# Twenty-six products that nobody reads, placed in waits of TensorE in a four-layer decoder

## The chip, the core and the metric

The kernel is one launch on one core of a Trainium2 chip. The metric is the device time of the launch in microseconds, the median of several runs. Five engines work beside each other: TensorE (PE in the rows; PEld is its load of a stationary operand), VectorE (DVE), ScalarE (ACT), GpSimd (POOL) and SyncE (SP), which issues the transfers. They meet by semaphores that the kernel's text names itself: every wait is written out by hand.

## The reference

Eight sequences of 128 tokens with 128 features pass through four layers. Each layer is an attention-like stage, a second stage that may look at a context, and a mixture of experts; each is added to `x` and gets the layer norm of `x`. All is float32.

```python
for layer in range(4):                      # 12 stages in a row
    x = x + attn[layer](layernorm(x))       # L1: a gated linear recurrence; L3: 10 chosen queries per head
    x = x + xattn[layer](layernorm(x), ctx) # L0, L1: softmax attention; L2: linear attention (elu + 1); L3: two products
    x = x + ffn[layer](layernorm(x))        # experts with 2 (L3: 1) of 8 chosen per token

# L0_xattn, the pattern of the softmax attentions: 16 heads of 8 features
q, k, v = split(x @ Wq.T), split(ctx @ Wk.T), split(ctx @ Wv.T)
scores = where(causal, q @ k.T / sqrt(8), -inf)
out = merge(softmax(scores) @ v) @ Wo.T
```

## The kernel before

**Layout.** `x` lies in SBUF as 128 tokens by 8 sequences times 128 features, and `ctxT` holds the context turned, 128 features by 1024 tokens. PSUM is used as eight tiles of 128x512 float32, `banks[0]` to `banks[7]`. A float32 product of 128x128 by 128x512 stands in the profile as two MATMUL rows of 128x512, so "x2" there is one such product.

**Order.** There is no scheduler. Each engine runs its functions in the order in which they are written, stage after stage, and an instruction whose wait is not met stops all that stands behind it on its engine. Some work of the next stage is written into the loops of the stage before (functions with `ahead` in the name).

**The attentions of layers 0 and 3** (`batches_pe`, line 915, and its partners on the other engines) loop over u = 0 to 9, one step per sequence and two to drain. At step u TensorE makes the scores of sequence u (four products with 32 rows each, L922, into banks 0 to 3), turns the exponentials of sequence u-1 (L939, banks 4 and 5), multiplies them by the values (L534, bank 6) and turns the sums back (L929). The scores of u wait for the masks of u-1 (`masked`, made by VectorE in L1037) in layer 0, and for `lowered` (VectorE, L1048) in layer 3. At u = 0 there is no u-1, so TensorE has nothing between the scores of the first sequence and those of the second. The hook `ahead(pe, u, "end")` is called at the end of each step.

**The recurrence of layer 1** (`layer1_recurrence_pe`, line 1829) mixes the recurrence's products with the key and value products of the next stage (`layer1_keys_values_pe(pe, i)`, L2023, i = 0 to 15) and its queries (L2030). Number 15 waits until ScalarE has emptied the bank that number 12 wrote (L2169). VectorE empties number 15 (L2171), then runs the scan of the recurrence (L1949 to L1955), and the recurrence's last product L1821 waits for that.

**The attention of layer 1** (`layer1_cross_pe`, line 2048) loops over v = 0 to 10, four heads of four sequences at a time. `EDGE_USES[v]` lists what else TensorE turns in step v (L2091): the values `("vh", n)` in steps 0, 2 and 3, and the results `("weighed", n)` in steps 6, 7 and 10. Each such group of four transposes into bank 7 waits until VectorE has emptied bank 7 of the last one (`freed`). In the list, n = 0 to 2 occur twice, as `vh` in step 0 and as `weighed` in steps 6 and 7.

**The second stage of layer 2** (`layer2_cross_pe`, line 2660) has a like loop: scores L2674, then sums of queries (L2683) and values (L2691). Its first scores wait for the queries, keys and values to be made positive and masked by VectorE, ScalarE and VectorE again.

**Layer 3's attention** gets its scores into `batches_pe` after a long stretch on VectorE that picks queries.

Of the kernel before, what the change touches and what calls it, by code (L numbers as in the profile page):

```python
# [21 lines left out]
BANK = 512  # L22
# [98 lines left out]
def build_program(nc, d, out):  # L121
    with ExitStack() as ctx:
# [179 lines left out]
        def turn_x_pe(pe, st, h, bank):  # L302
            n = norm[st]
            for j in range(4):
                b = 4 * h + j
                pe.wait_ge(*n["xc"](b + 1))
                o = pe.transpose(banks[bank][:, j * P:(j + 1) * P], xc[:, b, :], ident[:, :])
            o.then_inc(n["turned"].sem, 1)

        def keep_xnT(eng, who, st, h, bank):  # L310

# [1319 lines left out]


        def layer0_experts_ahead_pe(pe, u, point):
            if (u, point) == (7, "end"):
                pe.wait_ge(*a1s["masked"](4 * NB))
                turn_x_pe(pe, "L0_ffn", 0, 3)
            if (u, point) == (8, "heads back"):
                pe.wait_ge(*weights("L0_ffn"))
                pe.wait_ge(*norm["L0_ffn"]["xn0"](1))
                route_logits_pe(pe, e0, 0, W["L0_ffn_gate_w"][:, :], 2)  # L1640
            if (u, point) == (9, "heads back"):
                route_counts_pe(pe, e0, 0, 2)
# [182 lines left out]
        def layer1_recurrence_pe(pe):  # L1825
            pe.wait_ge(*weights("L1_attn"))
            recurrence_in_pe(pe, 0)
            pe.wait_ge(*weights("L1_xattn"))
            pe.wait_ge(*r1m[0].out(3))
            for i in range(4):  # L1830
                layer1_keys_values_pe(pe, i)
            recurrence_gates_pe(pe, 0)
            for i in range(4, 8):
                layer1_keys_values_pe(pe, i)
            turn_x_pe(pe, "L1_attn", 1, 2)
            pe.wait_ge(*r1m[0].out(7))
            recurrence_in_pe(pe, 1)
            recurrence_out_pe(pe, 0)
            for i in range(8, 12):
                layer1_keys_values_pe(pe, i)  # L1840
            recurrence_gates_pe(pe, 1)
            turn_x_pe(pe, "L1_xattn", 0, 4)
            for i in range(12, 16):
                layer1_keys_values_pe(pe, i)

            pe.wait_ge(*norm["L1_xattn"]["xn0"](1))
            pe.wait_ge(*r1m[1].out(7))
            layer1_queries_pe(pe, 0, 0)
            layer1_queries_pe(pe, 0, 1)
            pe.wait_ge(*kv1m.out(14))  # L1850
            layer1_queries_pe(pe, 0, 2)
            pe.wait_ge(*kv1m.out(15))
            layer1_queries_pe(pe, 0, 3)
            recurrence_out_pe(pe, 1)
# [180 lines left out]
        def layer1_cross_pe(pe):  # L2035
# [4 lines left out]
            for v in range(8 + 3):  # L2040
# [41 lines left out]
                for use, n in EDGE_USES[v]:  # L2082
# [8 lines left out]
                        o = pe.transpose(banks[7][:, j * P:(j + 1) * P], src, ident[:, :])  # L2091
                    o.then_inc(g["vh_turned" if use == "vh" else "heads_back"].sem, 1)
                    freed = g[use](n + 1)
                if v == 1:
                    pe.wait_ge(*kv1m.out(13))
                    turn_x_pe(pe, "L1_xattn", 1, 6)
# [562 lines left out]

        def layer2_cross_pe(pe):  # L2660
            g, m = c2g, c2m
            pe.wait_ge(*m.out(1))
            pe.wait_ge(*m.out(2))
            pe.wait_ge(*m.out(3))
# [362 lines left out]
        def layer3_attention_pe(pe):  # L3027
# [15 lines left out]
            pe.wait_ge(*g["wg_unit"](1))  # L3043
            pe.transpose(banks[7][0:GD, 3 * P:3 * P + NE], wg_unit[:, :], ident[0:NE, 0:NE]).then_inc(g["wg_turned"].sem, 1)
            pe.wait_ge(*g["wg_ready"](1))
            batches_pe(pe, a3s, a3h, a3["qT"], W["L3_attn_woT"][:, :], a3["vp"], "L3_attn", False, layer3_cross_ahead_pe)

        def layer3_attention_act(act):
# [172 lines left out]


        def layer3_cross_ahead_pe(pe, u, point):
            if (u, point) == (7, "end"):
                pe.wait_ge(*a3s["lowered"](3 * NB))
                pe.wait_ge(*a3s["exped"](4 * NB - 3))
# [314 lines left out]
```

## Time and profile before

| What | Value |
|---|---|
| Median of 3 runs | 1294.52 us (1293.5 to 1294.74) |
| The profiled execution, its own time | 1286.18 us |
| Span of its trace, first to last instruction | 1284.2 us |
| Mean granted TensorE clock | 0.896 of full speed |
| Busy: PE, PEld, DVE, ACT, POOL | 79%, 59%, 60%, 51%, 26% |
| DMA | 33 GB/s mean, 42.46 MB |

The granted clock is a share of 2.4 GHz: 1.00 is 2.4 GHz and 0.50 is 1.2 GHz, the only two levels; a value between them is a mix over the stretch. Times in rows are microseconds from the start of the span. The end of a row is its start plus its duration. The brackets at a row's end say how long the engine sat idle before it and who released it.

### The profile page before, as it was taken

What the parts mean: (1) busy time and instruction counts of PE and PEld (TensorE: products, weight loads), DVE (VectorE), ACT (ScalarE), POOL (GpSimd) and SP (SyncE); (2) the same over time, 40 slices, a digit from 0 to 9 for tenths busy, and PEclk for the clock granted to TensorE, in tenths of its full rate; (3) what the DMA queues carried; (4) which work ended last, traced back from release to release, by engine and by line L of the source; (5) the groups of instructions that cost most, each with busy time, mean ns of one, the idle gap of its engine ahead of it and who ended that gap; (6) DMA issues with size and microseconds to landing.
All of it is one profiled execution on the core that took longest, in us unless ns stands there. A gap on an engine that the chain in (4) does not pass through costs nothing. (4 is left out here: it accounts for less than half of the span.)

```text
span 1284.2 us, 22278 instructions
## 1 busy us (share of the span) xinstructions
PE 1010.8 (79%) x8221; PEld 758.4 (59%) x8221; DVE 771.8 (60%) x1870; ACT 656.8 (51%) x1688; POOL 337.2 (26%) x440
## 2 busy tenths in 40 slices
PE   6257877783779767779999989997789961878998
PEld 4224444352776355579976765775358850546898
DVE  4889995783323766752246665665777667764422
ACT  1168885561445646736538774775113223763433
POOL 2254542662222134410003331333410031111000
PEclk9689897896889778999999999999689995998999
DMA  7200000002555000020000000000120000000000
GB/s 246 85 1 1 2 1 18 1 1 66 150 166 198 1 1 2 2 99 1 1 2 1 2 2 1 2 2 33 79 107 26 1 1 0 2 1 1 1 1 17
DMA packets 31978, 42.46 MB, mean 33 GB/s; under 512 B 7592, under 2 KB 25632, under 8 KB 30592
## 3 DMA queue, kind: packets, MB, share of 16 engines
q1 hardware_dynamic: 30848, 38.95, 9.1%
q0 software_dynamic: 1024, 2.10, 0.5%
q8 instruction: 66, 1.08, 0.4%
q14 instruction: 40, 0.33, 0.1%
HBM read 35.54 MB, written 5.51 MB: 32 GB/s over the span
## 5 line engine op out<-in xcount | busy, mean ns | idle before, releaser
L1287 ACT ACTIVATE arena<-bank,w_L_ffn_b1T 128x512 f32<-128x512 f32 x128 | 86.9, 688 | 98.5 <-PE bank L1229 98.0
L1264 PEld LDWEIGHTS bank<-bufB,arena 128*128 128x128 f32 x1024 | 118.9, 192 | 2.4
L1264 PE MATMUL bank<-bufB,arena 128*128 128x128 f32 x1024 | 119.6, 275 | 0.0
L2525 ACT ACTIVATE arena<-arena 128x128 f32<-128x128 f32 x256 | 99.2, 390 | 20.0 <-DVE arena L2552 20.0
L293 POOL TENSOR_TENSOR norm_rstd<-norm_std,minus_half 128x4 f32<-128x4 f32 x24 | 25.4, 1060 | 316.0 <-DVE norm_std L288 316.0
L2536 POOL TENSOR_TENSOR arena<-arena 128x512 f32<-128x512 f32 x64 | 66.5, 1040 | 151.8 <-DVE arena L2585 151.8
L1324 DVE SCALAR_TENSOR_TENSOR x<-bank,gate_c,x 128x128 f32<-128x128 f32 x128 | 36.0, 344 | 114.9 <-PE bank L1264 114.7
L545 ACT ACTIVATE arena<-arena 128x128 f32<-128x128 f32 x256 | 80.3, 395 | 42.3 <-DVE arena L553 42.3
L1229 PE MATMUL bank<-x_high,w_low 128*128 128x512 f32 x200 | 85.7, 429 | 8.1 <-DVE w_low L1238 5.5
L1229 PE MATMUL bank<-x_high,w_high 128*128 128x512 f32 x200 | 81.1, 405 | 0.0
L1229 PE MATMUL bank<-x_low,w_high 128*128 128x512 f32 x200 | 81.0, 405 | 0.0
L2548 DVE SCALAR_TENSOR_TENSOR arena<-bank,bufA 128x512 f32<-128x512 f32 x64 | 43.8, 685 | 35.2 <-PE bank L2474 35.2
L2848 ACT ACTIVATE arena<-bank 128x512 f32<-128x512 f32 x36 | 21.6, 599 | 61.2 <-PE bank L1229 61.2
L514 PE MATMUL bank<-arena 128*128 128x512 f32 x64 | 37.3, 674 | 18.9 <-DVE arena L474 18.9
L2396 PE MATMUL bank<-xnT,bufA 128*128 128x512 f32 x96 | 50.7, 627 | 1.6 <-ACT arena L341 1.6
L341 ACT ACTIVATE arena<-bank 128x512 f32<-128x512 f32 x36 | 21.5, 596 | 58.7 <-PE bank L2396 39.3
L757 POOL TENSOR_TENSOR arena<-arena 128x512 f32<-128x512 f32 x32 | 33.8, 1057 | 64.4 <-DVE arena L876 64.4
L2445 PE MATMUL bank<-arena 128*64 128x128 f32 x512 | 42.1, 285 | 10.7 <-ACT arena L2516 10.5
L1229 PEld LDWEIGHTS bank<-x_high,w_low 128*128 128x128 f32 x200 | 39.4, 197 | 17.1 <-DVE w_low L1238 6.0
L2431 PEld LDWEIGHTS bank<-arena 128*128 128x128 f32 x256 | 36.7, 191 | 21.2 <-issue 14.1
L963 ACT ACTIVATE arena<-bank 128x512 f32<-128x512 f32 x64 | 36.7, 598 | 23.5 <-PE bank L939 23.1
L2525 ACT ACTIVATION_READ_ACCUMULATOR arena<-arena 128x1 f32 x256 | 48.3, 189 | 0.0
(489 smaller groups left out, 2555.6 us busy)
## 6 DMA issues: line engine op xcount, KB each, us to landing
bufB<-in_L_ffn_w SPq DMA_DIRECT2D x28, 256.0 KB
bufA<-in_L_ffn_w SPq DMA_DIRECT2D x2, 2048.0 KB, 9.8
bufB<-in_L_ffn_W SPq DMA_DIRECT2D x2, 2048.0 KB
bufB<-in_L_ffn_w SPq DMA_DIRECT2D x2, 2048.0 KB
bufA<-in_L_ffn_Wgu SPq DMA_DIRECT2D x1, 2304.0 KB, 9.0
bufA<-in_L_attn_Wqkv SPq DMA_DIRECT2D x1, 2048.0 KB, 8.8
rows<-blank SPq DMA_DIRECT2D x2, 960.0 KB, 6.9
results<-arena SPq DMA_DIRECT2D x6, 256.0 KB
```

The lines of the kernel that those rows point to most:

```text
L514: pe.matmul(banks[k % 2][:, :], qT[:, b * P:(b + 1) * P], m["kM"][k % 4].rearrange("p j t -> p (j t)"), start=True, stop=True).then_inc(s[ ...
L545: m = act.activation(tile[:, j * P:(j + 1) * P], tile[:, j * P:(j + 1) * P], ACT.Exp, bias=low[:, j:j + 1], scale=SCALE)
L963: act.activation(m["p"][n % 4], banks[4 + n % 2][:, :], ACT.Copy).then_inc(s["probs"].sem, 1)
L1229: m = pe.matmul(bank[:, :], a[:, ws], b[:, c], start=n == 0, stop=n == 2)
L1264: i = pe.matmul(bank[:, j * P:(j + 1) * P], h[:, f, j * P:(j + 1) * P], w2[:, u * FF + f * P:u * FF + (f + 1) * P], start=f == 0, stop=f = ...
L1287: act.activation(m["h"][k % 2][:, f, :], banks[f][:, :], ACT.Gelu, bias=b1[:, c:c + 1]).then_inc(g["hidden"].sem, 1)
L2396: o = pe.matmul(bank[:, :], w[:, c * P:(c + 1) * P], xnT[:, i * BANK:(i + 1) * BANK], start=True, stop=True)
L2431: o = pe.matmul(banks[7][:, u * P:(u + 1) * P], b2["oT"][k % 2][:, j * P:(j + 1) * P], b2_wo[:, c:c + P], start=False, stop=k == UNITS - 1 ...
L2445: o = pe.matmul(banks[5 + k % 2][64 * t:64 * t + 64, j * P:(j + 1) * P], b2["v"][gg % 2][:, 4 * u + 2 * j + r, :], b2["p"][(U0 + k) % 3][: ...
L2525: o = act.activation(tile, tile, ACT.Exp, bias=b2["mn"][n % 8][:, j:j + 1], scale=-1.0, accum_out=b2["sm"][n % 8][:, j:j + 1])
L2536: pool.tensor_tensor(tile, tile, bc(b2["rs"][n % 4], 2, P), ALU.mult).then_inc(g["over_sum"].sem, 1)
L2548: dve.scalar_tensor_tensor(tile, banks[r][:, :], -1.0 / np.sqrt(DH).item(), bias[:, h0:h0 + 4, :].rearrange("p h t -> p (h t)"), ALU.mult, ...
```

## The change

A helper makes `n` products of the identity by the first half of the context, 128x128 by 128x512 in float32, into a bank. It signals nothing and nobody reads the result. It is called at six places in the text: behind the scores of u = 0 in layers 0 and 3 (three products each), before key and value product 15 of layer 1 (five), behind each group of `EDGE_USES` with n below 3 (one each), and before the first scores of layer 2's second stage (nine). The last group runs six times, since n below 3 comes as `vh` and again as `weighed`, so 26 products are made in all. Two waits are written in for bank 6: `r1m[1].out(7)` before the five, and `a3m.out(4)` before layer 3's batches.

```diff
+        def keep_clock_pe(pe, bank, n):
+
+            for _ in range(n):
+                pe.matmul(banks[bank][:, :], ident[:, :], ctxT[:, 0:BANK], start=True, stop=True)
...
         def layer0_experts_ahead_pe(pe, u, point):
+            if (u, point) == (0, "end"):
+                keep_clock_pe(pe, 6, 3)
...
             turn_x_pe(pe, "L1_xattn", 0, 4)
-            for i in range(12, 16):
+            for i in range(12, 15):
                 layer1_keys_values_pe(pe, i)
+            pe.wait_ge(*r1m[1].out(7))
+            keep_clock_pe(pe, 6, 5)
+            layer1_keys_values_pe(pe, 15)
...
                     o.then_inc(g["vh_turned" if use == "vh" else "heads_back"].sem, 1)
                     freed = g[use](n + 1)
+                    if n < 3:
+                        keep_clock_pe(pe, 6, 1)
...
         def layer2_cross_pe(pe):
             g, m = c2g, c2m
+            keep_clock_pe(pe, 6, 9)
...
             pe.wait_ge(*g["wg_ready"](1))
+            pe.wait_ge(*a3m.out(4))
             batches_pe(pe, a3s, a3h, a3["qT"], W["L3_attn_woT"][:, :], a3["vp"], "L3_attn", False, layer3_cross_ahead_pe)
...
         def layer3_cross_ahead_pe(pe, u, point):
+            if (u, point) == (0, "end"):
+                keep_clock_pe(pe, 6, 3)
```

No other engine's order changes. On TensorE, at layer 1's attention in step v = 0, between the last scores and the scores of v = 1, this stood before (L2052 is a score, L2091 a transpose of values):

```order
L2052 MATMUL bank3<-bufA,arena 128x128
L2091 MATMUL bank7<-ident,bufA 128x128 x4
L2091 MATMUL bank7<-ident,bufA 128x128 [waits vh]
L2091 MATMUL bank7<-ident,bufA 128x128 x3
L2052 MATMUL bank0<-bufA,arena 128x128 [waits masked]
```

The second and third of these rows' pattern came three times there. Now (L2062 and L2101 are the same two lines, moved by the added text, and L313 is the helper's product):

```order
L2062 MATMUL bank3<-bufA,arena 128x128
L2101 MATMUL bank7<-ident,bufA 128x128 x4
L313 MATMUL bank6<-ctxT,ident 128x512
L2101 MATMUL bank7<-ident,bufA 128x128 [waits vh]
L2101 MATMUL bank7<-ident,bufA 128x128 x3
L2062 MATMUL bank0<-bufA,arena 128x128 [waits masked]
```

One product stands between a group of transposes and the next one's wait, three times. On TensorE in step v = 6 of the same loop the rows are now these (L2089 turns exponentials):

```order
L2089 MATMUL bank5<-ident,arena 128x128 x3
L2101 MATMUL bank7<-ident,bufA 128x128 [waits res,vh]
L2101 MATMUL bank7<-ident,bufA 128x128 x3
L313 MATMUL bank6<-ctxT,ident 128x512
L2101 MATMUL bank7<-ident,bufA 128x128 [waits weighed]
L2101 MATMUL bank7<-ident,bufA 128x128 x3
L313 MATMUL bank6<-ctxT,ident 128x512
L2062 MATMUL bank0<-bufA,arena 128x128 [waits masked]
```

The second L313 stands directly before the scores of v = 7; before the change the last transposes did.

## Rows read from the trace of the kernel before

**Rows 1.** The page, 40 equal slices of the span: TensorE's granted clock in tenths

```profile
PEclk9689897896889778999999999999689995998999
```

**Rows 2.** Windows: stretch, us, busy of PE, PEld, DVE, ACT, POOL, clock, DMA

```profile
230.50:240.70 10.20, 6.00 (x36) 3.20 (x36) 8.12 (x13) 4.69 (x8) 7.66 (x10) 0.50 0.01 2
240.80:288.40 47.60, 40.09 (x423) 24.10 (x420) 40.18 (x84) 34.67 (x67) 35.00 (x39) 1.00 0.00 1
466.10:493.20 27.10, 19.10 (x209) 15.45 (x212) 15.30 (x35) 9.04 (x18) 12.36 (x13) 0.50 0.01 1
899.60:913.00 13.40, 9.85 (x58) 4.52 (x58) 9.95 (x17) 1.15 (x3) 8.54 (x21) 0.50 0.40 170
1056.60:1097.40 40.80, 8.69 (x40) 4.33 (x41) 27.43 (x70) 14.80 (x22) 7.70 (x9) 0.50 0.00 0
```

**Rows 3.** Timeline, start of layer 0's second attention: start, us, engine, instruction, count

```profile
228.44 1.14 PE L922 MATMUL bank<-bufB 32*128 32x512 f32 x8 [1.48 <-DVE bufB L903]
234.70 2.09 PE L922 MATMUL bank<-bufB 32*128 32x512 f32 x8 [5.12 <-POOL bufB L903]
...
240.77 0.68 DVE L1037 TENSOR_TENSOR arena<-bank,causal 128x512 f32<-128x512 f32 x1
...
242.51 1.14 PE L922 MATMUL bank<-bufB 32*128 32x512 f32 x8
...
249.10 1.14 PE L922 MATMUL bank<-bufB 32*128 32x512 f32 x8
```

**Rows 4.** Timeline, end of layer 1's recurrence

```profile
441.62 7.11 PE L1811 MATMUL bank<-arena,w_L_attn_WgT 96*96 96x512 f32 x16
449.10 2.80 PE L2023 MATMUL bank<-ctxT,w_L_xattn_WvT 128*32 128x256 f32 x48
456.34 1.93 PE L2023 MATMUL bank<-ctxT,w_L_xattn_WvT 128*32 128x256 f32 x16 [4.44 <-ACT bufA L2169]
458.34 1.02 DVE L2171 TENSOR_TENSOR bufA<-bank,w_L_xattn_bv 128x512 f32<-128x512 f32 x1 [4.25 <-PE bank L2023]
464.15 2.13 PE L1821 MATMUL bank<-w_L_attn_WoT,arena 96*128 96x128 f32 x16 [1.88 <-DVE arena L1955]
```

**Rows 5.** Timeline, layer 1's attention, steps 0, 1, 6 and 7

```profile
473.35 1.11 PE L2091 MATMUL bank<-ident,bufA 128*128 128x128 f32 x4 [0.40 <-DVE arena L2198]
...
487.56 6.47 PE L2030 MATMUL bank<-xnT,w_L_xattn_WqT 128*32 128x128 f32 x128 [1.92 <-ACT xnT L341]
...
527.64 0.71 PE L2091 MATMUL bank<-ident,bufA 128*128 128x128 f32 x4 [0.90 <-DVE arena L2228]
528.29 1.17 PE L2052 MATMUL bank<-bufA,arena 8*128 8x128 f32 x32
529.48 0.69 DVE L2211 TENSOR_TENSOR arena<-bank,arena 128x512 f32<-128x512 f32 x1 [0.50 <-PE bank L2052]
```

**Rows 6.** Timeline, start of layer 2's second stage, and a later step

```profile
893.65 0.61 PE L2431 MATMUL bank<-arena 128*128 128x128 f32 x4
901.72 2.09 PE L2674 MATMUL bank<-bufB 32*128 32x512 f32 x8 [7.46 <-DVE bufB L903]
906.49 2.09 PE L2674 MATMUL bank<-bufB 32*128 32x512 f32 x8 [1.43 <-DVE arena L2772]
918.24 0.33 PE L2697 MATMUL bank<-ident,bufB 128*128 128x128 f32 x1 [2.24 <-DVE x L2786]
```

**Rows 7.** Timeline, layer 3's attention, and two full-width products at the lower clock

```profile
13.60 3.75 PE L349 MATMUL bank<-xnT,w_L_attn_Wq 128*128 128x512 f32 x4 [0.83 <-issue]
...
1085.00 2.09 PE L922 MATMUL bank<-arena 32*128 32x512 f32 x8 [1.20 <-DVE arena L903]
1092.38 2.09 PE L922 MATMUL bank<-arena 32*128 32x512 f32 x8 [5.29 <-DVE arena L1048]
```

**Rows 8.** Windows: a stretch with L2091 transposes alone, and the fall after 916.5

```profile
546.50:550.90 4.40, 2.37 (x16) 1.80 (x15) 1.65 (x6) 0.79 (x2) 0.00 (x0) 1.00 0.00 0
...
920.00:930.10 10.10, 7.91 (x80) 4.58 (x78) 7.21 (x13) 0.28 (x1) 4.86 (x15) 0.50 0.01 2
```

## The prediction

> **What bounds the kernel now.** I read first the page's slices, for TensorE's granted clock [rows 1]. A digit below 9 marks a slice in which part of the work ran at 1.2 GHz instead of 2.4. In the first half nearly every slice has some, in the middle none. The windows then say where the low stretches lie [rows 2]: 230.5 to 240.7 at the start of layer 0's second attention, 466.1 to 493.2 in layer 1's, 899.6 to 913.0 at the start of layer 2's second stage, 1056.6 to 1097.4 before and in layer 3's attention. In each the reader is to see a clock of 0.50, and beside it 1.00 in the steady part of the same attention, 240.8 to 288.4. Last I read the timeline for what TensorE did before each fall and for the duration of one instruction group at either level.
>
> The pattern is the same each time. TensorE waits for another engine: 5.12 us before 234.70 [rows 3], 4.44 us before 456.34 [rows 4], 7.46 us before 901.72 [rows 6], 5.29 us before 1092.38 [rows 7]. The work behind the wait is slow: eight score rows take 2.09 us at 234.70 and 1.14 us at 228.44 and 242.51 [rows 3]. Nothing else differs between them. So the change has to be priced by the work that follows each wait, at either clock, and only where another engine then waits for it.
>
> **What one product costs.** No row before has this very product. The nearest at 2.4 GHz is the eight products of L1811, 7.11 us for 16 rows, so 0.89 us each (96 rows of the array, the same 512 columns) [rows 4]. At 1.2 GHz it is L349: four rows, two products, 3.75 us, so 1.88 us each [rows 7]. All 26 together take about 23 us of TensorE at the high clock and 49 at the low one. What matters is whether they end before the wait they stand in.
>
> **Layer 0, three products.** The scores of u = 0 end at 229.58, the next start at 234.70 [rows 3]. At 2.4 GHz the products end at 229.58 + 3 x 0.89 = 232.25, hidden by 2.4 us. At 1.2 GHz they would end at 235.22, 0.5 us late. If the clock stays up, the scores of u = 1 take 1.14 instead of 2.09: 0.95 us, and VectorE masks those scores and paces what follows. More is possible: from 234.70 to 242.51 a step took 7.81 us, the next took 6.59 [rows 3], a difference of 1.22. And VectorE's last mask ended at 241.45 [rows 3], 1.06 us before the scores it allows; those were held by transposes at the low clock. So the gain lies between 0.95 and 0.95 + 1.06 = 2.0. I take the middle, 1.5.
>
> **Layer 1, five products.** They start when number 14 ends, 449.10 + 2.80 = 451.90, and end at 451.90 + 4.45 = 456.35, to be set against 456.34 [rows 4]: cost nothing, with nothing to spare. The wait written in before them is for ScalarE's copy of a gate whose product ended at 448.73 [rows 4], three microseconds earlier, so it is met. Number 15 then takes 2.80 / 3 = 0.93 instead of 1.93, a gain of 1.0. It counts in full: VectorE had idled 4.25 us for number 15 (L2171 at 458.34) and from there runs without a stop to the scan's end that L1821 waits for at 464.15 [rows 4]. At most 1.0, at least 0.
>
> **Layer 1's attention, six products.** Three stand in step 0. The waits of the second and third group of transposes are 0.40 us [rows 5], and a group takes 1.11 at the low clock, so VectorE paces them at 1.51 us. At 2.4 GHz a group (0.71 with its wait for the pipeline, by the row at 527.64) plus a product makes 1.60: on time within 0.1. At 1.2 GHz it makes 1.11 + 1.88 = 2.99, so each is 1.48 late, 2.96 for two, and the copies of VectorE behind them too. Against that stands the group of queries at 487.56: 6.47 us for 128 rows at the low clock [rows 5], and number 15's fall from 1.93 to 0.93 says that at the high clock it would be half. High from the start, that is up to 3.2 less. The ends are +2.96 and -3.2, nearly even, so I take 0 and keep both.
>
> The other three come in steps 6 and 7, with `weighed` n = 0 to 2. Two are hidden: the wait before 527.64 is 0.90 against 0.89 [rows 5], and n = 2 stands in a wait of the same kind. The one for n = 1 is not: the scores L2052 at 528.29 started without idle time behind the transposes, and VectorE idled 0.50 us for them at 529.48 [rows 5]. It moves them by one product: a loss of 0.87 to 0.89 us, and 1.88 at the low clock. I take 0.9.
>
> **Layer 2, nine products.** They start at 893.65 + 0.61 = 894.26 and end at 894.26 + 8.01 = 902.27, 0.55 us after 901.72 [rows 6]. The scores then take 1.14 instead of 2.09, the width of L922's, so they end 0.4 earlier. The second scores at 906.49 wait for VectorE's masks of the first and shift by the same 0.4; if the clock is still up they end 0.95 earlier again, 1.35 in all. The ends are 0.4 and, if the rest of 899.6 to 913.0 is fast too, one more such group, 2.3. I take 1.35.
>
> **Layer 3, three products.** Here the clock has been low since 1056.6, so they start slow, at 1085.00 + 2.09 = 1087.09. If it never rose they would end at 1092.73, 0.35 late against 1092.38 [rows 7]. If it rises while they run, they end early and the second scores take 1.14: 0.95 gained, since VectorE waits for them. I take 0.95; the ends are -0.35 (a loss) and 2.0 as in layer 0. The wait for `a3m.out(4)` is for a copy that ScalarE makes before ones already waited for, and costs nothing.
>
> **A rule weighed.** At 546.5 to 550.9 TensorE made nothing but four groups of L2091 transposes with pauses, and the clock stayed 1.00 [rows 8]. So transposes hold it here, and behind the products of layer 0 they count as work. The Trainium skill, page "TensorE: Matmul & The Clock Gate", section "Part 4: PE-mode transpose", says that transposes do not engage the high clock. By that rule layer 0's gain would be 0.95 instead of 1.5; by the row it is 1.5.
>
> **The sum.** -1.5 - 1.0 + 0 + 0.9 - 1.35 - 0.95 = -3.9 us. It is made against the profiled execution, 1286.18 us with a span of 1284.2. The median of the runs is 8.3 us above that, 0.65%. I have no row for that difference and put the same sum on the median: 1294.5 - 3.9 = 1290.6 us.
>
> **The rivals.** *The high clock does not survive the rest of the wait.* After layer 0's products 2.4 us of waiting remain. A wait of 1.88 us before 464.15 preceded the fall at 466.1 [rows 2, 4], and one of 2.24 before 918.24 [rows 6] preceded the low stretch from 920.0 [rows 8]. Against it: in layer 0 the full array works ahead of the rest. It gives layer 0 nothing, layer 2 0.4: -1.0 + 0.9 - 0.4 - 0.95 = -1.4, 1293.1 us. Chance 0.28, with all that ends within 2.6 us of before.
>
> *The products of layer 1's attention run at 1.2 GHz and delay it.* The clock was 0.50 from 466.1 to 493.2 [rows 2], and filling the earlier wait does not touch the 1.88 us before L1821. The price is 2.96 in step 0, 0.9 in step 6, 0.55 and 0.35 of products that overhang in layers 2 and 3, less 1.0 of number 15: +3.8, 1298.3 us. It decides when the second and third group of step 0 are late by 1.4 us each and layers 0, 2 and 3 return less than 1.0 in all: 2.8 + 0.9 + 0.9 - 1.0 - 1.0 = +2.6. Chance 0.12.
>
> *More than the sum.* The clock is held in step 0 of layer 1 and through its queries (-3.2), and layers 0, 2, 3 reach their upper ends (2.0, 2.3, 2.0): -1.0 - 3.2 + 0.9 - 6.3 = -9.6, 1284.9 us. What speaks against it is that the queries have a wait of 1.92 us right before them [rows 5], into which no product was put. Chance 0.10.
>
> *Transposes do not count.* In this kernel the products of layer 0 would then be followed only by scores with 32 rows, and the clock would fall after them: 0.55 less, so -3.35, 1291.2 us. The row at 546.5 speaks against it. The page named above would have it so. Chance 0.05.
>
> **How the numbers follow.** The forecast has 0.45, with its own range of -2.6 to -6.5 us: 1288.0 to 1291.9. A difference of 0.2%, 2.6 us, is about what a measurement of this kernel can tell from no change. Faster by more than that are the forecast, the transposes' case and the larger one: 0.45 + 0.05 + 0.10 = 0.60. The same: 0.28. Slower: 0.12. The range for 8 in 10 reaches over the case of no change to the edge of the slower one and into the larger one: 1286.0 to 1297.0.
>
> **What would show it.** In layer 0 the scores of u = 1 at 1.14 us, and a clock of 1.00 around 234 to 241. In layer 1 number 15 at about 0.93 with the product before it ending when it can start. In step 0 transposes of 0.6 to 0.7 us, not 1.1. In step 6 the scores L2062 about 0.9 later behind their transposes, and VectorE waiting 1.4 instead of 0.50. In layer 2 the first scores at 1.14, starting 0.5 late. In layer 3 a clock that rises before 1092. The prediction is wrong if the low stretches only move: a shift of all later work by a microsecond can make the clock fall in other waits, of which [rows 1] shows many in the first half, and neither sign of that can be read from this trace.

## The result, and the profile after

| | before | the change | ratio, 95% interval |
|---|---|---|---|
| Median, first comparison (5 runs each) | 1294.52 us (1290.41 to 1295.43) | 1285.15 us (1283.43 to 1288.78) | 0.9939 [0.9916, 0.9962] |
| The change once more (12 runs, 35 of before) | 1292.24 us | 1288.92 us (1279.84 to 1294.89) | 0.9979 [0.9957, 1.0000] |
| All runs of both, mean | 1292.18 us (87 runs) | 1287.84 us (17 runs) | -4.3 us (-2.5 to -6.2), -0.34% |

The kernel is faster. By how much, five runs can't tell: runs of one program scatter with a standard deviation of about 3 us. In each run the mean granted clock is known too, and within the 35 runs of before in the second row it goes with the time at a correlation of -0.8, so most of the scatter goes with the clock. Its mean over those runs was 0.893, and 0.908 for the change. The last row pools 5, 35 and 35 runs of before, 12 of before with an unused helper (below), and 5 and 12 of the change. The profiled execution of the change took 1288.78 us, that of before 1286.18, one of its quickest. So the two spans are no measure of the change, and the traces are compared place by place.

The page of the kernel after: the engines' busy time, and TensorE's granted clock in 40 slices, which answers [rows 1]:

```profile
PE 1028.8 (80%) x8273; PEld 767.6 (60%) x8273; DVE 772.9 (60%) x1870; ACT 656.3 (51%) x1688; POOL 337.1 (26%) x440
...
PEclk9689988995799898999999999999789995988999
```

TensorE has 52 MATMUL rows more (26 products of two) and is busy 18 us longer (1010.8 before). The mean clock rose from 0.896 to 0.909, yet four slices (6, 10, 11 and 36) are lower than before: low stretches also moved.

Windows of the kernel after, with the columns of [rows 2], over the same places:

```profile
466.00:476.00 10.00, 5.96 (x60) 4.22 (x60) 6.43 (x10) 0.81 (x2) 4.08 (x6) 1.00 0.01 2
476.10:479.30 3.20, 3.20 (x10) 2.01 (x10) 2.77 (x5) 1.33 (x3) 2.25 (x3) 0.50 0.00 0
...
486.30:496.40 10.10, 7.09 (x108) 6.25 (x112) 3.57 (x5) 5.53 (x12) 3.12 (x3) 0.50 0.01 2
896.50:909.40 12.90, 10.75 (x41) 4.43 (x39) 9.75 (x23) 3.14 (x5) 7.31 (x16) 1.00 0.70 276
909.60:912.80 3.20, 3.20 (x36) 2.35 (x37) 3.20 (x5) 0.24 (x1) 1.64 (x5) 0.50 0.00 0
1056.60:1093.70 37.10, 7.80 (x18) 3.34 (x19) 25.98 (x67) 13.77 (x19) 7.17 (x7) 0.50 0.00 0
```

The low stretches are shorter: 27 us in layer 1's attention became 3.2 and 10.1, layer 2's 13.4 became 3.2 at this place, and layer 3's ends at 1093.7, before the second scores.

Timeline of the kernel after, with the columns of [rows 3]. The added text moved lines: L922 is now L927, L939 L944, L2023 L2033, L2030 L2040, L2052 L2062, L2091 L2101, L2211 L2223, L2674 L2687. The rows answer in turn to [rows 3], [rows 4], [rows 5], [rows 6] and [rows 7]:

```profile
229.88 1.14 PE L927 MATMUL bank<-bufB 32*128 32x512 f32 x8 [1.48 <-DVE bufB L908]
230.95 2.84 PE L313 MATMUL bank<-ctxT,ident 128*128 128x512 f32 x6
236.15 1.25 PE L927 MATMUL bank<-bufB 32*128 32x512 f32 x8 [2.35 <-POOL bufB L908]
...
242.78 1.14 PE L927 MATMUL bank<-bufB 32*128 32x512 f32 x8
...
455.52 4.56 PE L313 MATMUL bank<-ctxT,ident 128*128 128x512 f32 x10
460.04 1.07 PE L2033 MATMUL bank<-ctxT,w_L_xattn_WvT 128*32 128x256 f32 x16
...
467.03 2.05 PE L1828 MATMUL bank<-w_L_attn_WoT,arena 96*128 96x128 f32 x16 [2.42 <-DVE arena L1965]
...
474.64 0.66 PE L2101 MATMUL bank<-ident,bufA 128*128 128x128 f32 x4 [3.01 <-DVE arena L2210]
475.13 1.07 PE L313 MATMUL bank<-ctxT,ident 128*128 128x512 f32 x2
476.16 1.11 PE L2101 MATMUL bank<-ident,bufA 128*128 128x128 f32 x4
477.06 1.91 PE L313 MATMUL bank<-ctxT,ident 128*128 128x512 f32 x2
478.77 0.91 PE L2101 MATMUL bank<-ident,bufA 128*128 128x128 f32 x4
479.61 1.17 PE L2062 MATMUL bank<-bufA,arena 8*128 8x128 f32 x32
...
532.23 1.02 PE L313 MATMUL bank<-ctxT,ident 128*128 128x512 f32 x2
533.18 1.17 PE L2062 MATMUL bank<-bufA,arena 8*128 8x128 f32 x32
534.37 0.69 DVE L2223 TENSOR_TENSOR arena<-bank,arena 128x512 f32<-128x512 f32 x1 [1.36 <-PE bank L2062]
...
896.49 7.89 PE L313 MATMUL bank<-ctxT,ident 128*128 128x512 f32 x18
904.31 1.14 PE L2687 MATMUL bank<-bufB 32*128 32x512 f32 x8
...
908.38 1.14 PE L2687 MATMUL bank<-bufB 32*128 32x512 f32 x8 [2.15 <-POOL bufB L908]
...
1089.51 4.95 PE L313 MATMUL bank<-ctxT,ident 128*128 128x512 f32 x6
1094.87 1.14 PE L927 MATMUL bank<-arena 32*128 32x512 f32 x8 [0.41 <-issue]
```

The reader is to see three things. The score rows behind products take 1.14 or 1.25 us where they took 2.09. A product costs 7.89 / 9 = 0.88 us at the high clock (L313 at 896.49), and 1.91 at the low one (477.06). And at 474.64 to 479.61 the products don't lie in a wait: TensorE has no idle time there, and the scores come late.

**Where the time came from.** The table gives the time from the start of one TensorE instruction to that of another, the same two in each kernel. "Single" is the kernel with that place's products alone. "Again" is the change's second trace.

The starts are taken to a nanosecond, so a difference can be 0.01 us off that of the rows shown.

| Place | before | after | again | single |
|---|---|---|---|---|
| Layer 0, scores of u = 1 to u = 2 | 7.81 | 6.64 | 6.15 | 6.15 |
| Layer 1, product 15 to L1821 | 7.81 | 6.99 | 6.98 | 6.97 |
| Layer 1's attention, scores of v = 0 to v = 1 | 9.71 | 10.60 | 10.61 | 10.49 |
| Queries L2030 to the next scores | 6.41 | 6.16 | 6.16 | 5.83 |
| Steps 6 and 7 (526.13 to 536.04 in before) | 9.91 | 10.87 | 10.88 | 10.88 |
| Layer 2, last transposes L2431 to first scores | 8.06 | 8.27 | 8.27 | 8.27 |
| Layer 2, scores of u = 0 to u = 1 | 4.78 | 4.08 | 4.08 | 4.08 |
| Layer 2, scores of u = 1 to u = 2 | 6.72 | 5.17 | 5.18 | 5.20 |
| Layer 3, scores of u = 1 to u = 2 | 7.40 | 6.43 | 6.43 | 6.43 |

Summed, after less before: -1.17 - 0.82 + 0.89 - 0.25 + 0.96 + 0.21 - 0.70 - 1.55 - 0.97 = -3.4 us.

**What whole stages keep of it.** The same measure from the start of each place to the end of its stage. "Without" are the kernels of the experiments below and before itself with no product at that place (single values or lowest to highest), "with" all those with the full-width ones that the change has there, and the last column is the difference of the two means:

| Stage | without | with | difference |
|---|---|---|---|
| Layer 0, scores of u = 1 to the end (6, 7 traces) | 64.0 to 66.3 | 61.8 to 66.1 | -0.2 |
| Layer 1's recurrence, product 14 to the next stage (6, 7) | 14.6 to 14.7 | 13.8 | -0.9 |
| Layer 1's attention to 536.04 in before (5) | 69.8 to 69.9 | five alone 70.4, six alone 71.8, both 71.9 | +0.6, +2.0, +2.1 |
| Layer 2's second stage (6, 6) | 52.7 to 54.9 | 51.2 to 52.8 | -1.4 |
| Layer 3's attention (6, 5) | 73.1 to 74.3 | 72.1 to 72.7 | -1.4 |

So part of each gain is given back inside its stage, most in layers 0 and 1: a low stretch that was avoided comes back later. The sum over the stages is -0.2 - 0.9 + 2.1 - 1.4 - 1.4 = -1.8 us. The 4.3 has an error of 1.8 us either way and the sum of the stages one of its own, so the two don't contradict each other. Whether the rest of the program, whose traces differ by some 5 us with no edit in it, gives the other 2.5 stays open.

### The profile page after: what moved, and what is told of

Same layout as the page of the kernel before. It is cut to its first block and busy times, and to the rows that moved or that the text cites. A ratio compares the mean times of both kernels' runs of the same rounds, so it can differ in the third digit from the quotient of the medians.

```text
span 1286.8 us, 22382 instructions
## 1 busy us (share of the span) xinstructions
PE 1028.8 (80%) x8273; PEld 767.6 (60%) x8273; DVE 772.9 (60%) x1870; ACT 656.3 (51%) x1688; POOL 337.1 (26%) x440
## 5 line engine op out<-in xcount | busy, mean ns | idle before, releaser
L519 PE MATMUL bank<-arena 128*128 128x512 f32 x64 | 39.9, 718 | 18.9 <-DVE arena L479 18.9
```

The lines of the kernel that those rows point to most:

```text
L519: pe.matmul(banks[k % 2][:, :], qT[:, b * P:(b + 1) * P], m["kM"][k % 4].rearrange("p j t -> p (j t)"), start=True, stop=True).then_inc(s[ ...
```

## The experiments

Theory 1: each place pays or costs by itself. A product is free while it ends before what TensorE waits for, costs its duration where no wait is left, and gives back what the next work saves at the high clock. Rival A: the clock isn't held, or the low stretches only move, and the places add up to nothing. Rival B: the gain comes from something other than the products, as the moved text. All kernels but the last ran against before in three series (medians of before 1292.3, 1292.24 and 1292.5 us, 25 to 35 runs each).

### Before with the helper, never called

```diff
+        def keep_clock_pe(pe, bank, n):
+            for _ in range(n):
+                pe.matmul(banks[bank][:, :], ident[:, :], ctxT[:, 0:BANK], start=True, stop=True)
```

> The kernel before with the unused helper in its text: no instruction differs. Both theories expect a ratio of 1.000 within 0.002; it shows how far two sets of runs of one program differ. Theory 1 (the terms of the prediction, read from one profiled execution, are the prices) says that this second trace has its low clock stretches at the same waits, with 455.8 to 459.2 and 466 to 493 among them. Theory 2 (where the low stretches fall differs from execution to execution, and the execution profiled before had fewer or cheaper ones than most, since it ran 8 us under the median) says that the trace's span is 1289 to 1294 us and that delays against the first trace appear in stages of identical code.

1292.11 us, ratio 1.0008 [0.9985, 1.0031]. Every local time of the table is the same within 0.04 us, and the low stretches lie in the same places up to 1138 us. Between these two traces of one program, though, the last stretch (1158.07 to 1273.11 in before) took 117.7 against 115.0 us. The text alone does nothing (rival B falls), and the traces' totals scatter by themselves.

### One place at a time

Layer 0:

```diff
+            if (u, point) == (0, "end"):          # layer0_experts_ahead_pe
+                keep_clock_pe(pe, 6, 3)
```

> Only the three products behind layer 0's first scores. Theory 1: -1.5 us (-0.95 to -2.0), ratio 0.9988, the second scores at 1.14 us. Theory 2: the same place gives about -1 to -2, but the total can move by 3 us either way with what the clock does elsewhere, so the ratio is 0.996 to 1.001.

1292.98 us, 0.9997 [0.9981, 1.0013]. Its timeline:

```profile
229.64 2.84 PE L313 MATMUL bank<-ctxT,ident 128*128 128x512 f32 x6
234.83 1.14 PE L927 MATMUL bank<-bufB 32*128 32x512 f32 x8 [2.35 <-POOL bufB L908]
...
240.97 1.14 PE L927 MATMUL bank<-bufB 32*128 32x512 f32 x8
```

The step fell to 6.15 us, 1.66 less; the step behind it grew by 0.21 (6.59 to 6.80). In the full change's first trace the clock fell inside the scores (1.25 us at 236.15) and the step took 6.64. To the end of the stage this trace is 2.3 us shorter than before's, more than the step gave, since no low stretch stands at the attention's end; that of the change is 1.9 us longer: there the low stretch of 288.5 to 291.9 in before was 284.8 to 295.1.

Layer 1's recurrence:

```diff
-            for i in range(12, 16):
+            for i in range(12, 15):
                 layer1_keys_values_pe(pe, i)
+            pe.wait_ge(*r1m[1].out(7))
+            keep_clock_pe(pe, 6, 5)
+            layer1_keys_values_pe(pe, 15)
```

> Only the five products before key and value product 15 of layer 1. Theory 1: -1.0 us, product 15 at 0.93 us instead of 1.93, the recurrence's last product 1.0 earlier, and a fall of the clock behind it as before. Theory 2: the same 1.0, and in addition the clock may hold through the start of layer 1's attention, for -2 to -4 us in all.

1291.7 us, 0.9986 [0.9964, 1.0008]. Product 14 to 15 took 4.83 us (4.82 before): the five cost nothing. Product 15 to L1821 took 6.97 us, 0.84 less, and the queries 5.46, 0.95 less. Then it is given back. A window of before over the same steps of the attention, then windows of this kernel and the one timeline row of TensorE that spans the second of them:

```profile
515.00:528.00 13.00, 9.53 (x167) 7.49 (x160) 11.23 (x19) 11.11 (x20) 9.25 (x10) 1.00 0.01 3
```

```profile
510.50:517.10 6.60, 6.60 (x69) 5.14 (x64) 5.29 (x9) 4.76 (x10) 4.26 (x5) 0.50 0.01 2
513.90:517.10 3.20, 3.20 (x16) 2.52 (x14) 2.95 (x5) 2.78 (x7) 2.36 (x4) 0.50 0.00 0
517.30:520.50 3.20, 3.20 (x73) 2.65 (x72) 1.95 (x3) 2.34 (x5) 1.24 (x2) 1.00 0.00 0
...
513.42 3.97 PE L2087 MATMUL bank<-ident,arena 128*128 128x128 f32 x16
```

In before all steps from 493.3 on ran at 1.00; here 510.4 to 517.2 is low, with TensorE busy throughout, and the stretch from the queries' end to step 6 took 33.60 us for 32.16. Of 1.79 us gained 1.44 are gone. The change's traces have the same later fall, shorter (520.4 to 523.8), 0.49 us. Before the fall at 510.4 TensorE had waited three times (0.34, 0.84 and 0.25 us), as it does in the same steps of before, where the clock stayed up.

The stretch ends in a way that bears on the rule weighed in the prediction: from 513.42 to 517.39 TensorE made nothing but transposes (L2087, 16 of them, back to back), and at 517.2 the clock went from 0.50 to 1.00. The same happened in two later kernels, at 521.5 in the one without layer 1's six and at 522.5 in the one with two products in the long wait.

Layer 1's attention:

```diff
                     freed = g[use](n + 1)
+                    if n < 3:
+                        keep_clock_pe(pe, 6, 1)
```

> Only the six products in layer 1's attention. Theory 1: step 0 late by up to 2.96 at the low clock, step 6 late by 0.9, against up to 3.2 less on the queries: near +0.9 us, ratio 1.0007. Theory 2: they bring the clock up within step 0, so the rest of the stretch from 466 to 493 (27 us at 1.2 GHz in the first trace) is short: -2 to -5 us, ratio 0.996 to 0.998.

1293.34 us, 1.0008 [0.9987, 1.003]. Its timeline in step 0:

```profile
469.63 0.66 PE L2096 MATMUL bank<-ident,bufA 128*128 128x128 f32 x4 [3.01 <-DVE arena L2205]
470.13 1.85 PE L313 MATMUL bank<-ctxT,ident 128*128 128x512 f32 x2
471.77 1.06 PE L2096 MATMUL bank<-ident,bufA 128*128 128x128 f32 x4
472.62 1.51 PE L313 MATMUL bank<-ctxT,ident 128*128 128x512 f32 x2
```

Here the clock fell at the first product and rose at the second, in the full change it fell one group later. Either way the step is late: +0.78 here, +0.89 there. Steps 6 and 7 are +0.97. The queries gained 0.58, the steps behind them lost 0.83. The stage is 2.0 us longer, though this part raised the runs' mean clock most of the five, from 0.893 to 0.899.

Layer 2, and layer 3:

```diff
         def layer2_cross_pe(pe):
+            keep_clock_pe(pe, 6, 9)
```

> Only the nine products before layer 2's second stage. Theory 1: -1.35 us (-0.4 to -2.3), the first scores at 1.14 us and 0.5 late. Theory 2: -1 to -4 us, since it removes one low stretch per execution whatever the others do.

1291.7 us, 0.998 [0.996, 1.0]. First scores +0.21, the next two steps -0.70 and -1.52. The whole stage took 52.71 us, 2.1 less than before's trace, but other kernels without products here had 53.0 to 53.2 as well.

```diff
+            pe.wait_ge(*a3m.out(4))               # ahead of layer 3's batches
...
+            if (u, point) == (0, "end"):          # layer3_cross_ahead_pe
+                keep_clock_pe(pe, 6, 3)
```

> Only the three products behind layer 3's first scores, with their wait. Theory 1: -0.95 us, the clock up before 1092 and the second scores at 1.14 us. Theory 2: the same place gives -1 to -2, the ratio lies between 0.998 and 1.0.

1290.8 us, 0.999 [0.9973, 1.0007]. The step fell from 7.40 to 6.43 us. The first step, 7.38, is as before.

The five parts' ratios are less than one by 0.03, 0.14, -0.08, 0.20 and 0.10%, 0.39% together, or 5.0 us. The plain means of the same runs give +0.2, -1.1, +1.4, -1.7 and -1.1 us, -2.4 together. No single one is beyond its interval, and the sum carries an error of some 0.2% either way, so both agree with the 4.3 us of all runs, and neither shows by itself that the parts add up. The mean clocks add up closely: +0.002, +0.002, +0.006, +0.004 and +0.001 over before in the same series give +0.015, and the change has +0.0155. Rival A, as "nothing adds up", falls by the steps of the table, which are the same alone and together, and by the change's own 4.3 us. Its milder form holds: low stretches also move, within the stages of layers 0 and 1.

### The change once more, and without layer 1's six

> The changed kernel as it stands, again, beside the parts. Theory 1 (terms as predicted): -3.9 us, ratio 0.997. Theory 2 (a gain larger than the terms, since most executions of before pay more at these waits than the one profiled): -6 to -9 us, ratio 0.993 to 0.9955, as the first comparison of the change gave.

1288.92 us, 0.9979 [0.9957, 1.0]: 3.7 us in the mean, as theory 1 said, and less than half of the first comparison's gain.

```diff
                     freed = g[use](n + 1)
-                    if n < 3:
-                        keep_clock_pe(pe, 6, 1)
```

> The change without the six products in layer 1's attention; the other twenty stand. Theory 1: these six cost about 0.9, so this is 0.9 us faster than the change (-4.8 against before). Theory 2: they shorten the long low stretch of layer 1's attention, so this is 1 to 3 us slower than the change.

1286.44 us, 0.9964 [0.9946, 0.9983]. Its timeline in step 0 and at the queries:

```profile
473.83 1.12 PE L2101 MATMUL bank<-ident,bufA 128*128 128x128 f32 x4 [0.40 <-DVE arena L2208]
...
488.05 5.53 PE L2040 MATMUL bank<-xnT,w_L_xattn_WqT 128*32 128x128 f32 x128 [1.92 <-ACT xnT L346]
```

The transposes are slow again and nobody is hurt: VectorE's copies pace them. Step 0 is back at 9.70, steps 6 and 7 at 10.01, and the queries take even less, 5.46 against 6.16 us; only the steps behind them are 0.94 longer. The six products cost 0.90 + 0.86 + 0.70 - 0.94 = 1.5 us by the traces. The two means differ by 1.4 us (1288.57 and 1287.22), but with an error of 2.8 us: the totals alone don't show that leaving them out helps.

### The same products with a quarter of the rows

```diff
-                pe.matmul(banks[bank][:, :], ident[:, :], ctxT[:, 0:BANK], start=True, stop=True)
+                pe.matmul(banks[bank][:, :], ident[0:32, :], ctxT[0:32, 0:BANK], start=True, stop=True)
```

> All 26 products with 32 rows instead of 128: the same columns and the same time on TensorE, a quarter of the array. Theory 1 (the gain is the clock, and what holds it is work in the array): in layer 0 the clock falls in the wait as it did before the change, the step from the second to the third scores takes 7.8 us again instead of 6.2 to 6.6, layer 3's 7.4 instead of 6.43, and the total is 0 to +2 us against before, since the hidden products' costs remain (0.9 twice in layer 1's attention, 0.2 in layer 2). Rival (any occupied TensorE holds the clock, or the gain is not the clock's): the same local times as the change, -4 us.

1299.87 us, 1.0055 [1.0036, 1.0075]: slower, by 7.4 us in the mean. Windows of it over layer 2's products, and over the start of layer 3's attention:

```profile
901.70:912.00 10.30, 10.30 (x21) 4.46 (x24) 7.36 (x19) 2.26 (x3) 5.30 (x11) 0.70 0.81 323
1066.30:1107.30 41.00, 13.79 (x46) 6.35 (x47) 27.63 (x70) 14.84 (x23) 7.86 (x9) 0.50 0.00 0
```

TensorE was busy without a pause from 901.70 to 912.00, and still the clock fell, at 905.9, while the products ran. In layer 1's recurrence too it fell under them, at 458.7, and product 15 came late. They end late and the scores come 10.25 us behind the transposes, not 8.27. Its timeline in layer 1's step 0:

```profile
477.22 2.07 PE L313 MATMUL bank<-ctxT,ident 32*128 32x512 f32 x2
```

The step took 12.77 us, 3.06 more than before: the 2.96 that the prediction gave as its upper end, 2 x 1.48. Over the places: layer 0 with its next step -1.0, products 14 to 15 +0.95, step 0 +3.06, queries -0.5, the steps behind them +0.7, steps 6 and 7 +0.97, layer 2 +2.2 + 1.6 - 0.7, layer 3 0: +7.3 us of the 7.4. The runs' mean clock was 0.8925, against 0.894 of before, so these are the price of 26 products without the gain. A busy TensorE wasn't enough; in layer 1's recurrence, layer 2 and layer 3 products over all the rows held or raised what those over 32 didn't. In layer 0 the expectation missed: the step took 6.67 us, not 7.8, as in the three traces of full products where the clock fell inside the scores (6.62 to 6.79). So layer 0 doesn't tell thin products from full ones. All this is one trace of the thin kernel; its ten runs agree in the total.

### Products in waits that have room

The six are out. Three products go before the last transposes of step 1 (a wait of 4.61 us in the change's trace), and in layer 3 two and five where TensorE waits for the picking of queries:

```diff
+                    if n == 3:                    # layer 1's attention, step 1
+                        keep_clock_pe(pe, 6, 3)
...
+            pe.wait_ge(*a3m.out(4))               # layer 3, behind the first turn
+            keep_clock_pe(pe, 6, 2)
...
+            keep_clock_pe(pe, 6, 5)               # layer 3, behind the count
```

> The change without the six of layer 1's attention, and with ten in other places: three before the last transposes of its step 1, two and five in the waits of layer 3's choice of queries. Theory 1: the first scores of layer 3 at 1.14 us instead of 2.09 and no worse second ones (-0.95), in layer 1 the 128 rows of queries shorter than 5.5 us (-1 to -2): -6.5 to -8 us against before, ratio 0.994 to 0.995. Rival (the clock falls again in the 1.9 us wait before the queries, and the products of layer 3 overhang): no better than without the ten, -4.7 us, ratio 0.9964.

1284.53 us, 0.9942 [0.9921, 0.9963], 7.9 us less than before in the mean. Its timeline at the queries and in layer 3:

```profile
482.66 4.11 PE L313 MATMUL bank<-ctxT,ident 128*128 128x512 f32 x6
...
489.53 1.95 PE L2040 MATMUL bank<-xnT,w_L_xattn_WqT 128*32 128x128 f32 x64 [1.88 <-ACT xnT L346]
491.97 1.95 PE L2040 MATMUL bank<-xnT,w_L_xattn_WqT 128*32 128x128 f32 x64 [0.49 <-ACT arena L2181]
...
1084.08 1.14 PE L927 MATMUL bank<-arena 32*128 32x512 f32 x8 [1.20 <-DVE arena L908]
...
1090.51 1.14 PE L927 MATMUL bank<-arena 32*128 32x512 f32 x8 [2.52 <-DVE arena L1053]
```

The 128 rows of the queries now take 1.95 + 1.95 where they took 6.47 [rows 5]; the block fell from 6.41 to 4.34 us. In layer 3 the first scores take 1.14 and the first step 6.43, not 7.38. Of the 1.1 us that the queries gain on the kernel without the six (5.46), 0.66 is given back in the steps behind them (34.25 for 33.59), where two low stretches of 3.4 us stand; layer 1's attention as a whole took 69.64 us, the least of all, though only 0.2 less than in before. Layer 3's attention took 71.75 us, also the least. The runs' mean clock is 0.912. The means against before went from -5.0 to -7.9 us; some 1.5 of the 2.9 is seen at the two places. The nearest comparison within one series is with the next kernel, which differs from the one without the six only by two products that change no local time: 3.7 us less, with an error of 2.2.

> The change without the six of layer 1's attention, and with two products in the one long wait of its step 0 (2.5 to 3.0 us). Theory 1 (the loss in step 0 came from products in waits of 0.40 us): the step from the first to the second group of scores takes 9.7 us as before the change, not 10.6; the clock holds past 476 or not, the total is -4.7 to -5.7 us. Rival (the loss came from the clock falling at 476 on its own): the step takes 10 us or more again.

```diff
-                    if n < 3:
-                        keep_clock_pe(pe, 6, 1)
+                    if (use, n) == ("vh", 0):
+                        keep_clock_pe(pe, 6, 2)
```

1287.31 us, 0.9971 [0.995, 0.9992]. Two products in the long wait of step 0 cost nothing (9.71 us) and bring nothing: 5.42 us for the queries against 5.46 without them. The clock fell at 474.7, inside the step, and the step was on time all the same, so the rival falls: what made step 0 late is products in waits of 0.40 us.

The last kernel is the one with the new places, with eight products in place of nine before layer 2's first scores, and two more behind the turn of unit 1:

```diff
-            keep_clock_pe(pe, 6, 9)
+            keep_clock_pe(pe, 6, 8)
...
+                    keep_clock_pe(pe, 4, 2)
```

> The kernel with products in new places (x2) and one more edit in layer 2: eight products in place of nine before the first scores, and two more behind the turn of unit 1, so that the step from unit 0 to unit 1 has some too. Theory 1 (a place pays where the products fit the wait and hold the clock for a step that TensorE's rows set): the first scores come 8.06 us behind the last transposes as in the kernel before, not 8.27 us (-0.2); the step u0 to u1 stays at 4.08 us or falls below it by up to 0.5, the step u1 to u2 is 3.8 to 5.2 us; in sum 0.2 to 1 us less than x2, ratio 0.9930 to 0.9945. Rival: the steps of this attention follow VectorE, and one product less before them lets the clock fall earlier: u0 to u1 back at 4.8 us and nothing gained, ratio 0.9940 to 0.9955.

1270.95 us against 1279.95 of before in its series, 0.9942 [0.9919, 0.9964]. Its timeline in layer 2, and at layer 3's second scores:

```profile
882.46 7.03 PE L313 MATMUL bank<-ctxT,ident 128*128 128x512 f32 x16
890.07 1.14 PE L2687 MATMUL bank<-bufB 32*128 32x512 f32 x8 [0.58 <-DVE bufB L908]
...
892.05 1.88 PE L313 MATMUL bank<-ctxT,ident 128*128 128x512 f32 x4
894.36 1.14 PE L2687 MATMUL bank<-bufB 32*128 32x512 f32 x8 [0.44 <-POOL bufB L908]
...
1076.05 2.09 PE L927 MATMUL bank<-arena 32*128 32x512 f32 x8 [2.52 <-DVE arena L1053]
```

The first scores come 8.06 us behind the transposes, as before; the ninth product was the overhang. But the next step took 4.29 us, not 4.08, so the two cancel. The ratio is that of the kernel without this edit. Neither theory's gain shows, and the clock was held to the third scores with eight as with nine.

This trace also shows what one trace per kernel hides, since outside layer 2 the kernel is the one with the new places. In layer 3 the clock fell at 1075.6, in the 2.52 us of waiting behind the three products; the second scores took 2.09 us and the step 7.94, not 6.43, and the attention 73.04 us, not 71.75. In layer 1 a low stretch lay on the queries (474.9 to 478.3): 5.76 us, not 4.34, and the attention took 70.86 us, not 69.64. So the local gains of the new places are what one trace had, not what each execution has.

## Why the prediction was right

Its sum was -3.9 us. All runs give -4.3 (-2.5 to -6.2), the places -3.4, of which whole stages keep less. The way was right: the products held or raised the clock in four of the five places, and the work behind them was as much shorter as priced. That the number fits so well is in part luck: one term was short by 1.6 us of cost and another by some 0.5 of gain, and what the stages gave back later was not in the sum at all.

The first comparison's 9.4 us put the median 0.85 us below the range, next to the 1284.9 us of the rival "more than the sum"; but in both traces of the change layer 1's attention was 2.1 us longer, where that rival needed it shorter. The second comparison gave 3.3. What the prediction lacked was the scatter of the kernel itself: with a standard deviation of 3 us, two medians of five runs differ by some 2.4 us for no cause. It took the difference between median and profiled execution for something to set aside, where it was this scatter.

- **One product**, 0.89 and 1.88 us: 0.88 and 1.91. Right.
- **Layer 0**, -1.5: -1.66 in the four traces where the clock held through the step, -1.0 to -1.2 in the three where it fell inside the scores (1.25, 1.47 and 1.89 us). The 1.5 is right for the step. Not foreseen: 0.2 comes back in the next step, and over the stage the means differ by 0.2 us only.
- **Layer 1's five**, -1.0 and no cost: -0.83, no cost. The wait for product 15 was filled to 0.01 us. Product 15 itself took 1.07 us, not the 0.93 that a third of 2.80 gave.
- **Layer 1's attention, step 0 and queries**, 0: +0.89 - 0.25 in the change, +0.78 - 0.58 in its own kernel, but 0.95 (queries 5.46, not 6.41) is had without these products, so they cost 1.6. This is the term that was mis-sized. It set a held clock for the queries against late transposes as if both came from these products. The queries gain from the five in the recurrence, and with the six a low stretch lies on them (486.3 to 496.4 in the windows). The lateness is between "on time within 0.1" and 2.96 because the clock was high for one product and low for the other. The clock fell inside step 0 in each trace with these products. The upper end of 3.2 less for the queries was too large as well: with the clock at 1.00 through all of them (the new places) the block was 2.07 shorter.
- **Steps 6 and 7**, +0.9: +0.96. VectorE waited 1.36 us at 534.37; the prediction said 1.4.
- **Layer 2**, -1.35: +0.21 - 0.70 - 1.55 = -2.0. Scores at 1.14 and a half microsecond of overhang in the products came as said, but the overhang cost 0.21, not 0.55, since the products started 0.45 us behind the transposes' start, not 0.61, and took 7.82 up to the scores, not 8.01. The third term is only partly the change's. Kernels without products here had 6.72, 6.71, 5.84, 5.81, 5.91 and 3.76 us for this step, those with nine 5.20, 5.17, 5.18 and three times 3.76. The means differ by 1.3, so -1.8 is the fairer figure, and over the whole stage -1.4.
- **Layer 3**, -0.95: -0.97. The three products took 4.95 us, between 3 x 0.88 and 3 x 1.91; the clock rose while they ran, and the scores started without a wait for VectorE in the row. The step was 0.97 us shorter in six traces, among them the one with the new places, where the clock was up before these products. In the last kernel, where it was up too, it fell in the wait behind them, and the step was 0.5 longer than in before.
- **A rule weighed.** The Trainium skill, page "TensorE: Matmul & The Clock Gate", section "Part 4: PE-mode transpose", would have given layer 0 0.95 instead of 1.5. The runs gave both: 1.66 in four traces, 1.0 to 1.2 in three. They don't decide it, since a fall inside the scores can't come from transposes that follow them. What speaks against the rule is the row in [rows 8], and more so the three traces in which the clock rose behind a stretch of transposes alone (3.97 us of them before 517.39 in the kernel with the five). So float32 transposes as this kernel makes them went with a rise of the clock, and the measurement decides against what the Trainium skill says there.

**The rivals.** "The clock does not survive the wait" fell as a rule, not in each case: 2.35 us of waiting lay behind layer 0's products, and the scores took 1.14 in four traces and 1.25, 1.47 and 1.89 in three, the last with a fall 0.2 us into them; behind layer 3's, in the last kernel, the clock did fall in the wait. "Products at 1.2 GHz in layer 1" happened in half, and in full with the thin products, +7.4 us. "More than the sum" needed the queries; a gain of 7.9 us came with other places. What the prediction named as the way to be wrong, that the low stretches only move, happened in part: in layer 1's attention 1.4 us of the five products' 1.8 came back in steps that ran at 1.00 before. Why the clock falls there is not shown; the waits before the fall were those of the kernel before. Traces of one program also differ by themselves, in one stage by 2.7 us.

## What to carry to other kernels

Fill a wait of TensorE only where the filler ends before what it waits for, and where what follows it is what others wait for: one row of the filler at either clock, and the wait's length, price each place before it is written. Work that another engine paces gains nothing from the high clock, and a filler there makes it late. Measure each place by the time between the two instructions that frame it, and then its stage to the end, since a low stretch avoided can come back in later steps. Take more than one trace: layer 3's three products gained 0.97 us in six traces and lost 0.5 in a seventh. The total of a few runs is too coarse for 1 us of 1290.

## What the runs showed of the hardware

- **One program, in another series, 12 us less.** In the last series before itself took 1279.95 us, 12.5 less than in the one ahead of it. The traces of the two variants show where: from layer 0's experts to layer 1's recurrence the last kernel took 141.1 us, the one with the new places 153.3, with the same code there. The chains of waits in the experts' first stretch, first of the kernel with the new places, then of the last one (engine, line, what it waited for: total us, times, longest):

```profile
POOL arena L1468 <- DMA results<-arena: 26.7, 1, 26.7
...
ACT arena L1558 <- remote: 13.0, 2, 8.3
```

```profile
POOL arena L1468 <- DMA results<-arena: 18.8, 1, 18.8
```

  GpSimd waited 8 us less for a store to land, and ScalarE's two waits on something that is no engine, 13.0 us, are gone. The first of them, 4.72 us, stands before the experts' first activation, whose weights and biases are loaded while it waits; that it is these loads is my reading, not shown. The store is the end of the experts' work, so its 8 us may be the same time seen again; how the 12.2 us divide was not worked out, and what made the waits shorter stays open.
- **Products over 128 rows held the clock where products over 32 did not.** With 32 rows it fell inside 10.3 us of TensorE without a pause; with 128 rows it stood at 1.00 for 7.89 us of products. In layer 0 the two did alike (6.67 and 6.62 to 6.79 us). A thin product is no cheaper: 2.07 us at the low clock.
- **The clock rose behind transposes alone.** Three traces have 3.95 to 3.97 us of float32 transposes back to back and the change from 0.50 to 1.00 within them.
- **A high clock is not time.** The six products of layer 1's attention raised the runs' mean clock by 0.006 and brought no time; the whole change by 0.0155, for 0.34%.
- **One step, four lengths.** Layer 2's scores of u = 1 to u = 2 took 3.76, 5.2, 5.8 or 6.7 us in kernels with the same text of this step, by where the clock fell; 3.76 came with nine products before it, with eight, and once with none.
